# Block-sparse attention stage of a fused kernel: first v through the ring of PSUM banks, constants awaited at use, maxima turned ahead of products, inverses and norms moved to earlier places

## The reference

```python
xn = _layernorm(x, axis=-1)
...
qkv = x @ w_qkv.T + b_qkv                      # x is xn here
scores = jnp.einsum('bhqd,bhkd->bhqk', q * scale, k) + mask
attn = jax.nn.softmax(scores, axis=-1)
out = jnp.einsum('bhqk,bhkd->bhqd', attn, v)
return out @ w_out.T + b_out
```

## Time and profile before

| | |
|---|---|
| median of 3 runs | 3223.01 us (3221.05 to 3223.15) |
| the profiled execution, its own time | 3223.25 us |
| span of the profile, first to last instruction | 3221.4 us |
| mean granted TensorE clock | 0.977 |
| busy share of PE, DVE, ACT, POOL over the span | 93%, 72%, 53%, 53% |
| this stage | from about 1272 to 1788 us, some 516 us |

### The profile page before, as it was taken

How to read it: one execution, slowest core, us unless ns; L and a number is a source line. 1 busy time by engine, 2 the same in 40 slices (tenths; PEclk the granted TensorE clock), 3 DMA queues, 4 the chain that set the end, 5 groups by cost and what they waited for, 6 DMA issues and landing times. The chain is left out here.

```text
span 3221.4 us, 46332 instructions
## 1 busy us (share of the span) xinstructions
PE 3012.0 (93%) x14220; PEld 1744.2 (54%) x14220; DVE 2332.8 (72%) x4168; ACT 1702.0 (53%) x3499; POOL 1706.3 (53%) x1106
## 2 busy tenths in 40 slices
PE   6999999999999987899999699999999999999997
PEld 2454545454545444455555366666666666666665
DVE  8999999999999987677775455666555655665553
ACT  4767686858686753344444244444444444444443
POOL 2666656666666655223332455555555555655552
PEclk9999999999999999899999799999999999999999
DMA  4767666766667666111010000000001100000000
GB/s 141 257 213 256 219 245 218 247 223 242 237 219 261 206 227 203 63 40 39 26 33 27 20 1 20 20 20 20 20 20 40 60 26 20 26 26 26 26 13 20
DMA packets 131294, 343.29 MB, mean 107 GB/s; under 512 B 14898, under 2 KB 57990, under 8 KB 131222
## 3 DMA queue, kind: packets, MB, share of 16 engines
q1 hardware_dynamic: 128918, 334.02, 30.4%
q10 hardware_dynamic: 2304, 8.39, 0.7%
HBM read 320.87 MB, written 21.50 MB: 106 GB/s over the span
## 5 line engine op out<-in xcount | busy, mean ns | idle before, releaser
L559 POOL TENSOR_TENSOR hb<-bcB,du 128x1024 f32<-128x1024 f32 x256 | 602.6, 2354 | 391.6 <-DVE hb L699 350.7
L688 DVE TENSOR_TENSOR_SCAN ps_dA<-ps_dA,hb 128x1024 f32<-128x1024 f32 x256 | 585.7, 2288 | 44.3 <-ACT ps_dA L914 44.3
L1226 PE MATMUL ps_y<-hb,ident 128*128 128x512 f32 x1024 | 491.6, 609 | 28.0 <-DVE hb L699 28.0
L2301 POOL TENSOR_TENSOR c_pr<-c_pr,c_inv 128x512 f32<-128x512 f32 (+1 forms) x256 | 237.3, 935 | 322.5 <-DVE c_inv L2418 322.5
L914 ACT ACTIVATE ps_dA<-delta,a_neg 128x511 f32<-128x511 f32 x512 | 330.0, 676 | 1.1
L1226 PEld LDWEIGHTS ps_y<-hb,ident 128*128 128x128 f32 x1024 | 189.9, 193 | 250.6 <-issue 187.5
L699 DVE TENSOR_TENSOR hb<-ps_dA,bcC 128x1024 f32<-128x1024 f32 x256 | 311.9, 1218 | 5.9
L2554 ACT ACTIVATE c_pr<-c_ps_s,c_negmax 128x256 f32<-128x256 f32 (+1 forms) x512 | 224.0, 452 | 149.2 <-DVE c_negmax L2411 124.8
L1741 ACT ACTIVATE b_pt<-b_ps_t 128x512 f32<-128x512 f32 x320 | 173.9, 595 | 223.3 <-PE b_ps_t L1849 222.4
L2278 POOL TENSOR_TENSOR c_q_cos<-c_q_cos,c_q_sin 128x1024 f32<-128x1024 f32 x64 | 151.0, 2359 | 248.5 <-DVE c_q_sin L2388 246.6
L2411 DVE CUSTOM_DVE_ANT_0 c_ps_s<-c_ps_s,c_mask 128x256 f32<-128x256 f32 (+1 forms) x512 | 188.5, 418 | 122.3 <-issue 122.3
(11 more groups left out here) (301 smaller groups left out, 5905.6 us busy)
## 6 DMA issues: line engine op xcount, KB each, us to landing
bcB<-bc_scratch SPq DMA_DIRECT2D x256, 512.0 KB, 4.4
bcC<-bc_scratch SPq DMA_DIRECT2D x256, 512.0 KB, 4.6
c_x<-stream_scratch SPq DMA_DIRECT2D x16, 512.0 KB, 4.7
c_xr<-stream_scratch SPq DMA_DIRECT2D x16, 512.0 KB, 3.9
rows<-in_x_dram SPq DMA_DIRECT2D x8, 512.0 KB, 5.3
sum<-in_x_dram SPq DMA_DIRECT2D x8, 512.0 KB, 7.5
x_scratch<-sum SPq DMA_DIRECT2D x8, 512.0 KB, 6.9
b_xb<-x_scratch SPq DMA_DIRECT2D x8, 512.0 KB, 4.6
```

Source lines behind the costliest of these rows:

```text
L559: pool.tensor_tensor(hb[:, s % RING, :, :], bcB[:, s % ROWS, :, :], bc(du[:, c % 2, :].unsqueeze(1), [P, NG, T]), ALU.mult)\
L688: dve.tensor_tensor_scan(flat(h_all), flat(h_all), flat(tile), 0.0, ALU.mult, ALU.add)\
L1226: last = pe.matmul(ps_y[:, :], W["ident"][:, :], hb[:, r % RING, i, :], start=False, stop=(g == GROUPS - 1 and i == NG - 1))
L2301: pool.tensor_tensor(rows, rows, bc(inv[:, u, :].unsqueeze(2), [P, 2, w]), ALU.mult)\
```

## The change

Six edits, all within `block_sparse_attention`:

1. v of batch 0 is projected in two halves into the ring of three banks, between the first scores (`project_first_v`), and ScalarE copies it out (`take_first_v`). TensorE's `project_v(0)` and VectorE's `take_v(0)` in `first` are gone. The two projections of q and k of half 1 are also set apart, after steps 4 and 6.
2. TensorE waits for the weights and the constants only ahead of the first projection, ScalarE for the weights only ahead of its first `take_qk`; before, each waited ahead of everything.
3. `turn_maxima` at step 8 of either half stands ahead of that step's `weigh`; before, behind it.
4. `invert` is one step sooner in half 0 (steps 2 to 5) and two steps sooner in half 1 (steps 1 to 4).
5. `statistics`, `root` and `norm` of a batch move about a batch sooner: for batch 1 into `first`, for batch b + 2 into half 1 of body b (steps 5 and 9).
6. The body of the last batch but one is now written out as well, since it has no batch b + 2; the loop runs five times in place of six.

```diff
-        AHEAD = [("x", h) for h in range(4)] + [("qk", m, keys) for m in range(DC) for keys in range(2)]
+        AHEAD = [("x", h) for h in range(4)] + [("qk", 0, 0), ("qk", 0, 1), ("v", 0), ("v", 1), ("qk", 1, 0), ("qk", 1, 1)]
...
-            body(0, False, True)
-            with eng.Fori(1, NB - 1) as b:
-                body(b, True, True)
-            body(NB - 1, True, False)
+            body(0, False, True, True)
+            with eng.Fori(1, NB - 2) as b:
+                body(b, True, True, True)
+            body(NB - 2, True, True, False)
+            body(NB - 1, True, False, False)
...
# GpSimd, body
-                if more:
-                    root(n)
...
                     mask(n, 1, 0, USES, b)
+                if more2:
+                    root(n + 1)
                 part_out(b, 1)
...
# VectorE, first
                     maximum(0, 0, k, k % 2)
+                    if k == 1:
+                        statistics(1)
+                    if k == 4:
+                        norm(1)
                 add_maxima(0, 0)
                 maximum(0, 1, 0, 1)
-                take_v(0)
                 maximum(0, 1, 1, 1)
...
# VectorE, body
-                    if more and k == 0:
-                        statistics(n)
-                    if more and k == 2:
-                        norm(n)
...
-                        if 3 <= k <= 6:
-                            invert(b - 1, 1, k - 3)
+                        if 2 <= k <= 5:
+                            invert(b - 1, 1, k - 2)
...
-                    if 3 <= k <= 6:
-                        invert(b, 0, k - 3)
+                    if 1 <= k <= 4:
+                        invert(b, 0, k - 1)
...
+                    if more2 and k == 5:
+                        statistics(n + 1)
                     if more and k == 8:
                         add_maxima(n, 0)
+                    if more2 and k == 9:
+                        norm(n + 1)
...
# TensorE
-            pe.wait_ge(s_w, 16 * 6)
-            pe.wait_ge(s_const, CONSTANTS)
...
+            def project_first_v(half):
+                use = FIRST["v", half]
+                free(0, use)
+                for t in range(2):
+                    at = (2 * half + t) * P
+                    for k in range(DC):
+                        last = pe.matmul(bank(use)[:, t * D:t * D + D], xT[:, k, at:at + P], w_qkv[:, k, 2 * D:3 * D],
+                                         start=(k == 0), stop=(k == DC - 1))
+                last.then_inc(filled.s, 1)
...
+                pe.wait_ge(s_w, 16 * 6)
+                pe.wait_ge(s_const, CONSTANTS)
...
-                    if k == 4:
-                        for keys in range(2):
-                            project_qk(0, 1, keys, 0, FIRST["qk", 1, keys], FIRST["x", 3])
+                    if k in (1, 3):
+                        project_first_v(k // 2)
+                    if k in (4, 6):
+                        project_qk(0, 1, k // 2 - 2, 0, FIRST["qk", 1, k // 2 - 2], FIRST["x", 3])
...
-                pe.wait_ge(qa_ready.s, qa_ready.at(0, 2))
-                project_v(0)
...
+                    if k == 8:
+                        if prev:
+                            pe.wait_ge(oT_ready.s, oT_ready.at(b, 0))
+                        turn_maxima(b, 1)
                     if k in (2, 4, 6, 8):
                         weigh(b, 0, (k - 2) // 2, uses, b)
```

More of the change, by code:

```diff
@@ L1383, in block_sparse_attention @@
         rstd_ready = S("b_rstd", 1, "pool")
-        done_ahead = (x_in, v_steps, ticks, mv_ready, g_steps, rstd_ready, xn_ready)
+        done_ahead = (x_in, v_steps, ticks, mv_ready, g_steps, rstd_ready, xn_ready, v_proj, v_taken)
         CONSTANTS, MASKS = 8, 3
@@ L1536, in first, with body @@
             def first():
-                for m in range(DC):
-                    for e in range(2):
-                        mask(0, m, e, FIRST, None)
-                pool.wait_ge(v_taken.s, v_taken.at(0, 1))
+                for e in range(2):
+                    mask(0, 0, e, FIRST, None)
+                root(1)
+                for e in range(2):
+                    mask(0, 1, e, FIRST, None)
                 for m in range(DC):
                     add_v_bias(m)
-            def body(b, prev, more):
+            def body(b, prev, more, more2):
                 n = b + 1
-                if more:
-                    root(n)
                 if prev:
@@ L1722, in _ @@
             seed(act, sems["act"], done_ahead)
-            act.wait_ge(s_w, 16 * 6)
             def take_x(n, h, b, use):
@@ L1736, in take_qk, with take_first_v @@
                                scale=1.0).then_inc(emptied.s, 1)
+            def take_first_v(half):
+                use = FIRST["v", half]
+                act.wait_ge(filled.s, used(0, use))
+                act.activation(v_rows[:, 2 * half:2 * half + 2, :], bank(use).rearrange("p (t d) -> p t d", t=2), ACT.Copy)\
+                    .then_inc(emptied.s, 1)
             def exponents(b, m, k, z, use):
@@ L1762, in first, with body @@
                     take_x(0, h, 0, FIRST["x", h])
-                for m in range(DC):
-                    for keys in range(2):
-                        take_qk(0, m, keys, 0, FIRST["qk", m, keys])
-            def body(b, prev, more):
+                act.wait_ge(s_w, 16 * 6)
+                for keys in range(2):
+                    take_qk(0, 0, keys, 0, FIRST["qk", 0, keys])
+                for half in range(2):
+                    take_first_v(half)
+                for keys in range(2):
+                    take_qk(0, 1, keys, 0, FIRST["qk", 1, keys])
+            def body(b, prev, more, more2):
                 uses = USES if more else LAST
@@ L1942, in body @@
                         swap_inverse(b - 1, 1)
-                    if k == 8:
-                        if prev:
-                            pe.wait_ge(oT_ready.s, oT_ready.at(b, 0))
-                        turn_maxima(b, 1)
                     if prev and k == 9:
@@ L1977, in body @@
                         weigh(b, 0, 4, uses, b)
+                    if more and k == 8:
+                        pe.wait_ge(oT_ready.s, oT_ready.at(b, 1))
+                        turn_maxima(n, 0)
                     if k in (2, 4, 6, 8):
@@ L1988, in body @@
                         swap_inverse(b, 0)
-                    if more and k == 8:
-                        pe.wait_ge(oT_ready.s, oT_ready.at(b, 1))
-                        turn_maxima(n, 0)
             def last(b):
```

## The result

The changed kernel takes 3201.32 us, median of 4 executions (3199.82 to 3203.95), against 3222.96 for the kernel before, a ratio on record of 0.9929 with a 95% interval of 0.9914 to 0.9944 (the two medians alone give 0.9933). By the medians it is 21.6 us faster. The prediction said 3194 in a range of 3184 to 3206: the direction is right and the time lies in the range, but the gain was put at 28.8, a third too high.

The account below looks back on a forecast made before the run. TensorE was taken to bound the loop, a chain through all engines the opening. Opening 10.0, six turns 15.6, body 0 2.2 and last body 1.0 sum to 28.8 us: 3223.25 becomes 3194, range 3184 to 3206.

Parts of the forecast that it names:

- Turns (15.6): Six turns, five in the loop and one written out, each to win 2.6 us by edits 3, 4 and 5.
- the ring and step 2's maximum: In a turn: bank wait cuts the norm's gain to 0.9 us; moved norm costs step 2's scores about 0.25.
- the like stop forecast at step 4: In a turn's half 1: reciprocals ahead of the maximum that step 4's scores wait for, costing 0.25 us.
- Everything behind moves up by 2.4.: Opening, up to the first scores: transposes run while constants are set, projections start sooner, gaining 2.4 us.
- First scores to body 0 (7.6): Later opening: 32.2 us falls to 24.6, gaining 7.6; bounds 21.3 if VectorE sets the length, 29.6 if half-clock TensorE does.
- Body 0 has the norm, a swap and one stop for queries: 2.2.: First body, ahead of the loop: these three savings together gain 2.2 us.
- My signs of being wrong: Turn over 57.5 us, opening's clock under 0.6, or the first body's scores beginning past 1314.
- Last body (1.0): Body of the last batch: it keeps the swap and output projection gains, 1.0 us.
- The opening is TensorE's: Rival, opening: clock stays low, stretch lasts 29.6 us, gain 5.0 instead of 10.0, time 3199; chance 0.15.
- VectorE is no bound in the loop: Rival claimed VectorE becomes the loop's bound: two new stops of 1.0 us each, time 3204; chance 0.13.
- GpSimd's root was never late: Slower rival, end of half 1: root holds VectorE's queue and delays maxima, time 3230; chance 0.03.
- the stops didn't give all they hold: Rival claimed they do: turns win 3.6 to 3.9 us, opening reaches its lower bound, time 3184; chance 0.12.

Follow-up runs that it names:

- e2_loop: The kernel before with edits 3 to 6 alone, the opening's order kept except for batch 1's statistics and norm; median 3208.53 us, ratio 0.9957.
- e3_fill_late: The changed kernel with seven added matmuls without use in TensorE's late stops of the opening; median 3199.3 us, ratio 0.9925.
- e1_opening: The kernel before with edits 1 and 2 alone; median 3221.3 us against 3222.49, ratio 0.9985.
- e4_fill_all: e3_fill_late with added matmuls also between the first transposes and projections and between those and the first scores; median 3193.86 us, ratio 0.9907.

## Why the prediction was right, and where it was off

- **Turns (15.6).** Right: 15.4. The waits named are gone, the ring and step 2's maximum are late next, with 0.37 and 0.24 where the prediction had about 0.3 and 0.25; the like stop forecast at step 4 is not there. By edit the terms were low by some 0.1 to 0.3 and the overlap between them, 0.43, wasn't counted; the two errors met, and that the sum fits to 0.2 us is luck in part. I had no view of that overlap: I should have walked the turn once with all edits in place and not each against the kernel before.
- **"Everything behind moves up by 2.4."** Off. The projections start when predicted, but behind a stop of 1.83, at half clock, and take 1.40 longer. Measured 1.1. The kernel before had the low clock there as well, but later projections, which ran partly after it had risen; starting sooner meant having more of them at 1.2 GHz.
- **First scores to body 0 (7.6).** 8.5 measured in the first profile, nearer the lower bound than I took it, and 7.3 in the second. With the term above 9.6 against 10.0 in the first, two errors of about one us that cancel; that is luck. With the stops filled the stretch takes 21.88, close to the lower bound of 21.3 that VectorE's work gave: what lay above it was TensorE's clock.
- **"Body 0 has the norm, a swap and one stop for queries: 2.2."** This term failed most: -2.8 measured in the first profile, 5.0 off, the largest share of the shortfall, and -0.5 in the second. From the first `score_keys` to the first `divide` it is 49.16 before, 51.95 and 49.70 after, and 48.05 in the three programs with fillers. So the edits themselves are worth 1.1 there, half of what I gave them (1.7 in `e2_loop`, without edits 1 and 2), and the low clock takes 3.9 or 1.7: in the first profile body 0 began on a clock at half until about 1320. In the kernel before the low clock lay under the projection of v, 1308 to 1316, ahead of body 0. I asked what the clock does within the stretch that I shortened, and not what it hands over to the next one. My signs of being wrong looked there only, too: a clock of 0.82 up to body 0 (under 0.6 would have been the sign) and body 0 at 1310.04 raised none.
- **Last body (1.0).** 1.4 in one execution and a loss of 4.3 in another of the same program. That this term is a draw is the likely reason why the median gain (21.6) is below that of the first pair of profiles (23.4); only profiled executions show it.
- **The rivals.** "The opening is TensorE's" named the right resource and a price close to the truth (3199), but mostly the wrong place: from 1290 to about 1306 the stretch was at full clock, and the loss lay at its two ends and in body 0. VectorE is no bound in the loop, GpSimd's root was never late, and the stops didn't give all they hold.
- **The rule that spoke against v in the ring.** In the rows the clock was already at half when v's first half began (1288.21), came back to full during it, stayed there through v's second half and the projections of half 1, and fell at the two stops behind them; with those filled it didn't fall. The stretch took 23.8 and 25.0 us in the two profiles and not the 29.6 of that rule. The Trainium skill ("TensorE: Matmul & The Clock Gate", "A second HAM failure mode: psum-queue depth-cycling") puts such swings down to short idle times between groups of matmuls. The trace agrees with that much: the clock fell at idle times (3 us in two stops, then 0.50), and not at the going round the banks.

Left open is what decides whether the clock falls at a given stop, in the last body above all; the same 2.75 ahead of the first scores was followed by 0.59 in the changed kernel's first profile and by 1.00 in `e3_fill_late`. The Trainium skill ("TensorE: Matmul & The Clock Gate", "What's actually happening") says that the same kernel can have a different number of matmuls at the low clock at its start from one execution to the next; here the difference lies in the middle of the program. The two profiles of the changed kernel agree (0.57 and 1.00 over the same work), but nothing here shows what sets it. Also open: in `e1_opening` a turn is 58.9 to 59.0 in place of 58.84, so that six cost 0.9 more, though the loop's code is the same.

## What to carry to other kernels

When an edit moves or shortens a stop of TensorE, read the granted clock behind the stop, in what comes next: half clock there cost 3.9 us in a body whose own edits were worth 1.1. A few matmuls without use in a stop, where nothing waits for TensorE, are cheap insurance. With them in the tail too, the time also repeated better: 0.7 us between four executions in place of 4; with fillers in the opening alone (`e4_fill_all`) it was still 6.3. Compare profiles by segments between places that both programs have, and profile the same kernel twice before a segment's difference is put down to an edit.

## What the runs showed of the hardware that I had not expected

One program at the same place of its work was granted 2.4 GHz in one execution and mostly 1.2 GHz in another, a difference of 5.66 us in a body of 57, while its loop repeated to 0.01 us. In the six us ahead of the fall TensorE had been busy for 4.67 in both. The last body is where TensorE stops for ScalarE again and again without the next batch's work between, and extra matmuls there went with full clock and with executions within 0.7 us of each other. Eight fp32 projection instructions (128x512) took 3.67 us at full clock and 6.75 from a start at half.
